# The inputs of a selective scan joined with the scan in one block, and its later step sizes made from broadcast rows

## The chip, the cores and the metric

The kernel runs on one core of one Trainium2 chip. The metric is the time of one execution on the device in microseconds; lower is better. The kernel is written engine by engine: TensorE (PE), VectorE (DVE), ScalarE (ACT), GpSimd (POOL) and SyncE (SP, which only issues transfers here) each have an instruction stream of their own and wait for each other on semaphores.

## The reference

The whole network has four layers, each a mixer and a feed-forward part, each followed by `x = layernorm(x + f(x))`, on activations of 8 sequences x 256 tokens x 128 channels. The change is in the mixer of the second layer, a selective scan:

```python
xz = x @ W_in                                   # 128 -> 2 x 256
x_inner, z = split(xz)
xc = silu(causal_depthwise_conv(x_inner, 4 taps) + conv_b)
x_ssm = xc @ W_xproj                            # 256 -> 1 + 16 + 16
delta = softplus(x_ssm[:, :1] * w_dt + b_dt)    # one raw step size a token, 256 channels
h_t = exp(delta * A) * h_{t-1} + delta * B_t * xc
y = (sum over 16 states of C_t * h_t + xc * D_param) * silu(z)
out = y @ W_out
```

## The kernel before

Each stage is one block: all engines meet at a barrier at its start and end. `stage_scan_inputs` (L1229) computes `xc` and `silu(z)` for all eight sequences, `stage_scan` (L1306) the rest. Channels lie on the 128 partitions in two halves (`c` = 0, 1), tokens along the free dimension.

Inputs, per sequence i: TensorE makes four 128x256 products in four banks (L1256; fp32, so two passes each in the trace). ScalarE copies the two x halves behind three zeros into `x_padded` (L1268), makes the first tap (L1271), the two `silu_z` (L1277) and, after VectorE's six taps (L1302, three per half, each on top of the last), the two `xc` (L1282).

Scan: one step n handles state k = n % 16 of sequence i = n // 16, 128 steps in all. ScalarE makes exp(delta * a) into a bank (`decay`, L1558, two per step), GpSimd multiplies `delta_x` with a broadcast row of B (`inject`, L1377), VectorE scans both (L1648). Even states are read out by tokens: TensorE turns them (L1434), ScalarE scales them by C (L1569), TensorE adds them up (L1463). Odd states: TensorE spreads a row of C (L1450), VectorE multiplies (L1658), TensorE adds (L1467). Rings of 4 injects, 3 decays and 4 states tie the engines together. Per sequence there are also `gate`, `step`, `stats` and `normalise` on VectorE, `project` and `turn_back` on TensorE, `rstd_of` on GpSimd.

The step sizes go by four groups of two sequences. `project_in(g)` (L1403) gives 33 rows `x_ssm`, which ScalarE (`keep`, L1526) or VectorE (group 1, L1640) copies to SBUF; `step_size(g, c)` (L1411) spreads row 0 times `w_dt` over the partitions in a bank. From that bank ScalarE takes |v + b| (`magnitude`, L1530) and VectorE max(v + b, 0) (`top`, L1613). ScalarE then takes exp(-|.|) (`below_one`, L1535) and ln(1 + .) (`log_of`, L1540), each of which needs another table, and VectorE adds both and multiplies with `xc` (`step`, L1625 and L1627). Group 0 is done before the first scan, group 1 around it, groups 2 and 3 by the dictionary `LATE` between steps 2 and 12; the logarithms of groups 1 to 3 are taken together at step 18.

SyncE stores rows 1 to 16 of a group to DRAM (`rows_out`, L1353, 32 KB) and loads them back spread over all partitions, four states of a sequence at a time (L1364, 512 KB, chunk q of 32, four buffers); chunk q waits for the injects of chunk q - 4. At its end each stage's SyncE stream runs `ready_next` (L102): it clears the semaphores of the next stage's pool and raises each by one. There are two pools used in turn, of 60 and of 36 semaphores; a stage's signals are taken from its pool in order.

Of the kernel before, what the change touches and what calls it, by code (L numbers as in the profile page):

```python
# [16 lines left out]
F32 = mybir.dt.float32  # L17
I32 = mybir.dt.int32
BF16 = mybir.dt.bfloat16
ALU = mybir.AluOpType  # L20
# [3 lines left out]
P = 128  # L24
# [1204 lines left out]
def stage_scan_inputs(nc, net, io, xc, sz):  # L1229

    with ExitStack() as ctx:
        sb = lambda name, shape: ctx.enter_context(nc.sbuf_tensor(net.name(name), shape, F32))
        PAD = NCONV - 1
        xp, acc = sb("x_padded", [P, 2, 2, PAD + L]), sb("conv", [P, 2, 2, L])
        s = open_stage(nc, net, f"clear:1 xz:{4 * B} x_padded:{2 * B} silu_z:{2 * B} first:{2 * B} taps:{2 * (NCONV - 1) * B} xc:{2 * B}")
        bank = net.bank
        seq = lambda i: slice(i * L, (i + 1) * L)
        bank_of = lambda i, m: bank[4 * (i % 2) + m]
        with nc.Block() as block:
            @block.sync  # L1240
            def _(sp):
                ready_next(sp, net)

            @block.gpsimd
            def _(pool):
                pool.memset(xp[:, :, :, :], 0.0).then_inc(s.clear.sem, 1)

            @block.tensor
            def _(pe):
                pe.wait_ge(net.ld_w, net.w_ready)  # L1250
                for i in range(B):
                    for m in range(4):
                        if i >= 2:
                            read, c = (s.x_padded, m) if m < 2 else (s.silu_z, m - 2)
                            pe.wait_ge(read.sem, read.at(0, 2 * (i - 2) + c + 1))
                        pe.matmul(bank_of(i, m)[:, 0:L], net.w_in[:, m * P:(m + 1) * P], net.xT[:, seq(i)], start=True, stop=True).then_inc(s.xz.sem, 1)  # L1256

            @block.scalar
            def _(act):
                act.wait_ge(net.ld_w, net.w_ready)  # L1260
                act.wait_ge(s.clear.sem, s.clear.at(0, 1))

                def pad(i):
                    for c in range(2):
                        act.wait_ge(s.xz.sem, s.xz.at(0, 4 * i + c + 1))
                        if i >= 2:
                            act.wait_ge(s.taps.sem, s.taps.at(0, 2 * (NCONV - 1) * (i - 1)))
                        act.activation(xp[:, i % 2, c, PAD:PAD + L], bank_of(i, c)[:, 0:L], ACT.Copy).then_inc(s.x_padded.sem, 1)  # L1268
                    for c in range(2):
                        act.wait_ge(s.x_padded.sem, s.x_padded.at(0, 2 * i + c + 1))  # L1270
                        act.activation(acc[:, i % 2, c, :], xp[:, i % 2, c, 0:L], ACT.Identity, scale=net.conv_w[:, c, 0:1], bias=net.conv_b[:, c:c + 1])\  # L1271
                            .then_inc(s.first.sem, 1)

                def gates(i):
                    for c in range(2):
                        act.wait_ge(s.xz.sem, s.xz.at(0, 4 * i + c + 3))
                        act.activation(sz[:, c, seq(i)], bank_of(i, 2 + c)[:, 0:L], ACT.Silu).then_inc(s.silu_z.sem, 1)  # L1277

                def conv(i):
                    for c in range(2):  # L1280
                        act.wait_ge(s.taps.sem, s.taps.at(0, 2 * (NCONV - 1) * i + 2 * (NCONV - 2) + c + 1))
                        act.activation(xc[:, c, seq(i)], acc[:, i % 2, c, :], ACT.Silu).then_inc(s.xc.sem, 1)  # L1282

                pad(0)
                for i in range(B):
                    gates(i)
                    if i + 1 < B:
                        pad(i + 1)
                    conv(i)

            @block.vector
            def _(dve):
                dve.wait_ge(net.ld_w, net.w_ready)
                for i in range(B):
                    at = 2 * (NCONV - 1) * i
                    for j in range(1, NCONV):
                        for c in range(2):
                            if j == 1:
                                dve.wait_ge(s.first.sem, s.first.at(0, 2 * i + c + 1))
                            else:  # L1300
                                dve.wait_ge(s.taps.sem, s.taps.at(0, at + 2 * (j - 2) + c + 1))
                            dve.scalar_tensor_tensor(acc[:, i % 2, c, :], xp[:, i % 2, c, j:j + L], net.conv_w[:, c, j:j + 1], acc[:, i % 2, c, :], ALU.mult, ALU.add)\  # L1302
                                .then_inc(s.taps.sem, 1)
# [2325 lines left out]
```

## Time and profile before

| | us |
|---|---|
| median of 3 runs | 1767.58 (1765.85 to 1769.92) |
| the profiled execution | 1780.49 |
| its span, first to last instruction | 1778.8 |
| TensorE busy in the span | 1519.8 (85%) |
| VectorE, ScalarE, GpSimd busy | 1009.0, 863.8, 632.8 |
| inputs of the scan, start to last `xc` | 538.05 to 563.62 |
| first scan instruction, last | 580.08, 810.21 |

The trace gives each instruction's start and duration, and for each idle stretch of an engine what ended it. Sums over a stage say which engine was busy, not which one decided; for that one looks at who waited for whom in that stage. "PEclk" is the granted clock of TensorE as a share of 2.4 GHz. A line such as `x4` merges neighbouring instructions of the same kind.

### The profile page before, as it was taken

The page shows a single profiled execution, that of the slowest core. Times are in us where ns is not written, and L with a number is a line of the kernel's source. Part 1 is how long each engine was busy: PE and PEld are TensorE (multiplying, and loading weights), DVE is VectorE, ACT ScalarE, POOL GpSimd, SP SyncE. Part 2 cuts the span into 40 slices and gives each one's busy share as a digit, 9 for nine tenths or more (in the row PEclk, how much of TensorE's full clock was granted, in tenths as well). Part 3 has the DMA queues.
Part 4 walks back from the last instruction along what each step waited for, and adds up shares of the span by engine and source line. Part 5 has one row for each costly group of instructions (what it writes and reads, how often), then busy time and mean ns, then how long its engine had stood idle before and what let it go on. Part 6 is the DMA issues. An engine that isn't in the chain of part 4 may idle for free. (4 is left out here: it accounts for less than half of the span.)

```text
span 1778.8 us, 31127 instructions
## 1 busy us (share of the span) xinstructions
PE 1519.8 (85%) x11198; PEld 1107.1 (62%) x11199; DVE 1009.0 (57%) x2370; ACT 863.8 (49%) x1903; POOL 632.8 (36%) x707
## 2 busy tenths in 40 slices
PE   4689978799886999996839999899996799778996
PEld 2356655466573566775837877787875476545664
DVE  6656536666375789995035554466645122535555
ACT  5455544565357677772425444544443132235552
POOL 3497603877140667772130000100013601511113
PEclk8889999899998899998959999999997899969998
DMA  7300000000000645635234000000000101300000
GB/s 219 117 10 16 13 7 2 14 13 13 13 1 14 92 65 77 78 59 121 71 89 130 1 0 1 1 1 1 1 1 6 59 26 30 37 4 2 2 2 25
DMA packets 75272, 63.65 MB, mean 36 GB/s; under 512 B 25367, under 2 KB 62790, under 8 KB 75142
## 3 DMA queue, kind: packets, MB, share of 16 engines
q1 hardware_dynamic: 65142, 53.53, 13.9%
q0 software_dynamic: 3072, 6.30, 1.8%
q10 hardware_dynamic: 6928, 2.12, 0.6%
q8 instruction: 79, 1.29, 0.3%
q14 instruction: 51, 0.42, 0.1%
HBM read 48.09 MB, written 9.57 MB: 32 GB/s over the span
## 5 line engine op out<-in xcount | busy, mean ns | idle before, releaser
L1377 POOL TENSOR_TENSOR inject<-delta_x,b_rows 128x512 f32<-128x512 f32 x128 | 159.5, 1269 | 80.2 <-DMA b_rows<-b_rows_dram 42.9
L1648 DVE TENSOR_TENSOR_SCAN state<-bank,inject 128x512 f32<-128x512 f32 x128 | 150.3, 1205 | 6.6 <-POOL inject L1377 3.3
L2085 POOL TENSOR_TENSOR ve<-mv,eps 128x1 f32<-128x1 f32 x32 | 6.1, 190 | 336.4 <-DVE mv L2233 336.4
L1558 ACT ACTIVATE bank<-delta,a_neg 128x255 f32<-128x255 f32 x256 | 109.0, 472 | 12.8 <-DVE state L1648 12.3
L3347 DVE TENSOR_REDUCE top<-bank 128x2 f32<-128x512 f32 (+1 forms) x96 | 61.8, 685 | 72.3 <-PE bank L3049 51.5
L2194 ACT ACTIVATE Z<-bank 128x512 f32<-128x512 f32 x64 | 34.7, 595 | 127.8 <-PE bank L2147 127.8
L2171 ACT ACTIVATE U<-bank 128x512 f32<-128x512 f32 x128 | 74.7, 593 | 41.8 <-PE bank L2108 40.7
L611 POOL TENSOR_TENSOR rotated<-rot_cos,rot_sin 128x512 f32<-128x512 f32 x56 | 70.8, 1269 | 52.4 <-DVE rot_sin L917 52.4
L617 POOL TENSOR_TENSOR inv_norm<-sum_sq,neghalf 128x16 f32<-128x16 f32 x28 | 82.0, 2929 | 4.2 <-POOL sum_sq L615 0.3
L1463 PEld LDWEIGHTS bank<-tabs,by_token 128*128 128x128 f32 x512 | 67.8, 196 | 24.9 <-issue 15.0
L654 PE MATMUL bank<-wqkv,hT 128*128 128x512 f32 x128 | 68.5, 665 | 14.7 <-ACT hT L815 11.3
L1569 ACT ACTIVATE by_token<-bank,c_cols 128x256 f32<-128x256 f32 x128 | 53.6, 469 | 50.8 <-PE bank L1434 50.5
L1467 PE MATMUL bank<-x_work,tabs 128*128 128x512 f32 x128 | 73.7, 658 | 0.0
L3260 ACT ACTIVATE prob<-bank 128x384 f32<-128x384 f32 x128 | 53.2, 501 | 37.0 <-PE bank L3077 37.0
L1463 PE MATMUL bank<-tabs,by_token 128*128 128x128 f32 x512 | 69.1, 279 | 0.0
L914 DVE TENSOR_TENSOR rot_cos<-bank,rope 128x512 f32<-128x512 f32 x64 | 43.8, 684 | 40.0 <-ACT squares L820 29.1
L2796 DVE TENSOR_TENSOR shared_hid<-shared_gate,bank 128x512 f32<-128x512 f32 x32 | 21.8, 686 | 65.7 <-PE bank L2648 27.4
L820 ACT ACTIVATE squares<-bank 128x512 f32<-128x512 f32 x64 | 38.0, 598 | 43.1 <-PE bank L654 23.3
L622 POOL TENSOR_TENSOR rotated<-rotated,inv_norm 128x512 f32<-128x512 f32 x56 | 57.2, 1042 | 2.2
L842 ACT ACTIVATE prob<-bank 128x512 f32<-128x512 f32 x64 | 34.7, 595 | 44.4 <-PE bank L701 44.4
L2968 POOL CAST k<-moe_w 128x512 bf16<-128x512 f32 x16 | 9.8, 610 | 116.3 <-ACT moe_w L3251 111.4
L663 PE MATMUL bank<-tabs,rotated 128*128 128x128 f32 x256 | 40.2, 292 | 12.6 <-DVE rot_sin L917 8.4
(564 smaller groups left out, 4163.2 us busy)
## 6 DMA issues: line engine op xcount, KB each, us to landing
b_rows<-b_rows_dram SPq DMA_DIRECT2D x32, 512.0 KB, 9.1
v<-v SPq DMA_DIRECT2D x32, 130.0 KB, 2.3
slots<-zero SPq DMA_DIRECT2D x10, 256.0 KB, 3.6
rows<-slots SPq DMA_DIRECT2D x10, 256.0 KB, 4.3
moe_w<-in_L_ffn_rg_dram SPq DMA_DIRECT2D x1, 2048.0 KB, 8.5
moe_w<-in_L_ffn_ru_dram SPq DMA_DIRECT2D x1, 2048.0 KB, 13.9
wqkv<-in_L_ffn_wqkv_dram SPq DMA_DIRECT2D x2, 768.0 KB
slots_out<-y SPq DMA_DIRECT2D x8, 160.0 KB, 2.1
```

Of the source, the lines that this page charges most:

```text
L611: pool.tensor_tensor(rot[:, p, m, :], rc[:, m % 2, :], rs[:, m % 2, :], ALU.add).then_inc(s.added.sem, 1)
L617: pool.tensor_tensor(flat(rn), flat(ss), net.neghalf[:, 0:2 * LH], ALU.pow).then_inc(s.inv_norm.sem, 2)
L622: pool.tensor_tensor(r, r, rn[:, m, :].unsqueeze(2).to_broadcast([P, LH, LDH]), ALU.mult).then_inc(s.roped.sem, 1)
L654: pe.matmul(to, hT[:, p, tok(t)], w[:, j * INNER:(j + 1) * INNER], start=True, stop=True).then_inc(s.qk_ps.sem, 1)
L1377: pool.tensor_tensor(dB[:, n % R, :, :], dx[:, :, seq(n)], both(b_all[:, q % 4, n % CH, :]), ALU.mult).then_inc(s.inject.sem, 1)
L1463: last = pe.matmul(sum_bank(i)[:, c * L + t * P:c * L + (t + 1) * P], hcT[:, j % RT, t, c * P:(c + 1) * P], ident, start=(k == 0 and t == ...
L1467: last = pe.matmul(sum_bank(i)[:, :], ident, flat(hc[:, j % R, :, :]), start=False, stop=(k == NS - 1))
L1558: last = act.activation(dA[n % RD][:, c, 1:L], delta[:, c, i * L + 1:(i + 1) * L], ACT.Exp, scale=a_neg[:, c, k:k + 1])
L1569: last = act.activation(hcT[:, j % RT, t, :], turn_bank[:, t * 2 * P:(t + 1) * 2 * P], ACT.Copy, scale=c_cols[:, TPB * i + t, k:k + 1])
L1648: dve.tensor_tensor_scan(flat(h[:, n % R, :, :]), flat(dA[n % RD]), flat(dB[:, n % R, :, :]), 0.0, ALU.mult, ALU.add).then_inc(s.state.sem, 1)
L2171: act.activation(U[:, m % 2, 4 * (g - 1):4 * g, :], bank[n % 2][:, :].rearrange("p (h t) -> p h t", h=4), ACT.Copy)\
L3347: dve.tensor_reduce(to, M[u % 2].rearrange("p (c k) -> p c k", c=count), AX.X, ALU.max).then_inc(s.maxed.sem, 1)
```

## The change

The two stages become one. `stage_scan_inputs` is emptied, and its work stands at the head of each engine's stream in `stage_scan`. The x products go to banks 3 to 6, each behind three columns that are zeroed once, and ScalarE and VectorE take all taps straight from the bank; `x_padded` is gone, and `conv` lies in a part of `x_tok`. The z products use the two halves of bank 7. All four `project_in` are issued among or right behind the inputs, through bank 2. Group 0's step sizes are made as before, but in the middle of the inputs. For groups 1 to 3 TensorE makes no step sizes: `rows_out` stores row 0 as well (17 rows), SyncE waits for its landing and loads row 0 spread over the partitions into `delta_x` (`step_rows`, 256 KB), ScalarE takes |row * w + b| from there at steps 5 to 10, and GpSimd makes row * w + b behind the injects 10, 12 and 14 (`top`); the max with 0 moves into `step`. `below_one` of groups 1 to 3 stands at steps 13 to 15, the logarithms at step 17. The third decay bank gets its zero column after `step(0)`. The transfers' semaphores now come from the stage's pool; as one stage fewer runs before the scan, the pools swap places, and have 44 and 60 semaphores.

```diff
-OTHER_SIGNALS = 36
+OTHER_SIGNALS = 44
-    net.pools = (net.pool, [sem(f"other_signal_{k}") for k in range(OTHER_SIGNALS)])
+    net.pools = ([sem(f"other_signal_{k}") for k in range(OTHER_SIGNALS)], net.pool)
...
 # SyncE
-                    sp.dma_start(b_dram[:, group_of(g)], ssm[1:1 + NS, group_of(g)]).then_inc(b_out[g], 16)
+                    sp.dma_start(rows_dram[:, group_of(g)], ssm[0:1 + NS, group_of(g)]).then_inc(b_out[g].sem, 16)
+                def step_rows(g):
+                    sp.wait_ge(b_out[g].sem, b_out[g].at(0, 16))
+                    sp.dma_start(dx[:, 0, group_of(g)], rows_dram[0, group_of(g)].partition_broadcast(P)).then_inc(rows_of[g].sem, 16)
...
-                    if q in (4, 6, 8):
-                        rows_out(q // 2 - 1)
+                    if q in (2, 3, 4):
+                        rows_out(q - 1)
+                        step_rows(q - 1)
...
 # GpSimd
+                def top(g):
+                    pool.wait_ge(s.abs.sem, s.abs.at(0, 2 * g + 2))
+                    for c in (1, 0):
+                        pool.tensor_scalar(dx[:, c, group_of(g)], dx[:, 0, group_of(g)], w_step[:, c:c + 1], net.b_dt[:, c:c + 1], ALU.mult, ALU.add)\
+                            .then_inc(s.top.sem, 1)
...
                 for n in range(LAST):
                     inject(n)
+                    if n in (10, 12, 14):
+                        top(n // 2 - 4)
...
 # TensorE
+                for i in range(4):
+                    inputs(i)
                 project_in(0)
+                inputs(4)
                 for c in range(2):
-                    step_size(0, c)
-                columns(early, bank[2])
+                    first_step_size(c)
+                columns(early, cc_bank)
+                inputs(5)
                 project_in(1)
-                for c in range(2):
-                    step_size(1, c)
+                inputs(6)
+                inputs(7)
+                project_in(2)
+                project_in(3)
...
 # ScalarE
+                for i in range(B):
+                    gates(i)
+                    if i + 1 < B:
+                        first_tap(i + 1)
+                    conv(i)
+                    if i == 2:
+                        keep(0)
+                    if i == 3:
+                        for c in range(2):
+                            magnitude(0, c)
+                    if i == 5:
+                        keep(1)
+                keep(2)
                 act.activation(a_exp[:, :, :], net.a_log[:, :, :], ACT.Exp).then_inc(s.a_exp.sem, 1)
...
                 below_one(0)
                 log_of(0, 1)
+                keep(3)
...
-                    if n < 2:
-                        magnitude(1, n)
-                    if n == 2:
-                        below_one(1)
...
+                    if 5 <= n < 11:
+                        magnitude(1 + (n - 5) // 2, (n - 5) % 2)
+                    if 13 <= n < 16:
                         below_one(n - 12)
-                    if n == 18:
+                    if n == 17:
                         for g in range(1, groups):
                             log_of(g, groups + g)
...
 # VectorE
-                    dve.tensor_tensor(delta[:, :, of], dx[:, :, of], delta[:, :, of], ALU.add).then_inc(s.delta.sem, 1)
+                    dve.scalar_tensor_tensor(delta[:, :, of], dx[:, :, of], 0.0, delta[:, :, of], ALU.max, ALU.add).then_inc(s.delta.sem, 1)
...
+                for i in range(B):
+                    taps(i)
+                    if i == 4:
+                        for c in range(2):
+                            first_top(c)
+                        columns(0, early, cc_bank)
...
                 step(0)
+                dve.wait_ge(s.ssm.sem, s.ssm.at(0, groups))
+                dve.memset(dA[RD - 1][:, :, 0:1], 0.0).then_inc(s.first.sem, 1)
```

## Rows read from the trace of the kernel before

**Rows 1.** Windows: us of each engine (instructions), PEclk, DMA share, GB/s.
```profile
core 0 of [0], span 1778.8 us
...
538.05:563.62 25.57, 17.68 (x64) 13.76 (x64) 20.34 (x48) 23.23 (x65) 0.95 (x1) 0.83 0.00 1
563.62:580.08 16.46, 12.06 (x24) 3.38 (x24) 4.35 (x13) 10.84 (x16) 1.30 (x2) 0.71 0.25 48
580.08:615.78 35.70, 34.34 (x146) 19.30 (x147) 29.05 (x32) 24.15 (x54) 22.86 (x19) 0.88 0.57 87
615.78:650.28 34.50, 31.75 (x149) 21.54 (x148) 26.51 (x34) 25.88 (x55) 20.41 (x18) 0.86 0.43 68
677.92:704.78 26.86, 26.86 (x151) 18.97 (x150) 26.79 (x36) 19.94 (x49) 20.77 (x18) 1.00 0.54 80
```
**Rows 2.** Timeline of the hand-over: start, us, instruction [idle before, releaser].
```profile
562.81 0.81 ACT L1282 ACTIVATE xc<-conv 128x256 f32<-128x256 f32 x2 [0.58 <-DVE conv L1302]
...
567.55 0.59 ACT L1526 ACTIVATE x_ssm<-bank 33x512 f32<-33x512 f32 x1 [2.15 <-PE bank L1403]
...
570.93 1.06 ACT L1535 ACTIVATE delta<-delta 128x1024 f32<-128x1024 f32 x1
...
572.01 1.28 ACT L1540 ACT_TABLE_LOAD   x1
...
575.33 0.67 DVE L1625 TENSOR_TENSOR delta<-delta_x,delta 128x512 f32<-128x512 f32 x1
...
577.40 2.46 ACT L1558 ACTIVATE bank<-delta,a_neg 128x255 f32<-128x255 f32 x6
578.78 4.93 POOL L1377 TENSOR_TENSOR inject<-delta_x,b_rows 128x512 f32<-128x512 f32 x4 [39.78 <-DMA b_rows<-b_rows_dram]
```
**Rows 3.** Groups by line, 580.08 to 615.78: busy, mean ns, idle before.
```profile
L1403 PE MATMUL bank<-xc,w_xproj 128*33 128x512 f32 x8 | 5.5, 829 | 0.0
...
L1411 PE MATMUL bank<-x_ssm,w_dt 1*128 1x512 f32 x8 | 4.5, 640 | 0.0
L1613 DVE TENSOR_SCALAR delta_x<-bank,b_dt 128x512 f32<-128x512 f32 x6 | 4.5, 746 | 6.2 <-ACT delta L1530 6.2
```
**Rows 4.** Timeline at the end of the first stage.
```profile
43.34 13.59 SPq L295 DMA_DIRECT2D slots<-zero  x10
...
55.61 0.60 ACT L425 ACTIVATE xT<-bank 128x512 f32<-128x512 f32 x1 [0.26 <-PE bank L344]
...
59.81 0.52 POOL L598 MEMSET hT<- 128x512 f32 x1 [19.65 <-POOLq L278]
```
**Rows 5.** Timeline: a three-operand instruction from PSUM, and the taps.
```profile
532.26 0.48 DVE L1205 SCALAR_TENSOR_TENSOR z<-bank,b,both 128x256 f32<-128x256 f32 x1 [0.52 <-PE bank L1139]
...
544.55 17.82 DVE L1302 SCALAR_TENSOR_TENSOR conv<-x_padded,conv_w,conv 128x256 f32<-128x256 f32 x40 [0.93 <-ACT conv L1271]
```
**Rows 6.** Timeline: TensorE's inputs, C columns, and a projection, at full clock.
```profile
551.29 1.99 PE L1256 MATMUL bank<-xT,w_in 128*128 128x256 f32 x8 [0.66 <-ACT silu_z L1277]
...
570.11 1.06 PE L1415 MATMUL bank<-tabs,x_ssm 33*128 33x16 f32 x8
...
599.21 1.91 PE L1403 MATMUL bank<-xc,w_xproj 128*33 128x512 f32 x4
```
**Rows 7.** Groups of GpSimd by line and shape, whole span.
```profile
L1377 POOL TENSOR_TENSOR inject<-delta_x,b_rows 128x512 f32<-128x512 f32 x128 | 159.5, 1269 | 80.2 <-DMA b_rows<-b_rows_dram 42.9 <-DVE state L1648 37.3
...
L622 POOL TENSOR_TENSOR rotated<-rotated,inv_norm 128x512 f32<-128x512 f32 x56 | 57.2, 1042 | 2.2
...
L1056 POOL TENSOR_TENSOR both<-x_work,xT 128x256 f32<-128x256 f32 x8 | 5.9, 732 | 0.1
...
L2992 POOL TENSOR_SCALAR x_tok<-x_tok,t_mv,t_rstd 128x128 f32<-128x128 f32 x6 | 5.0, 833 | 0.0
```
**Rows 8.** L1364 (b_rows) issued 570.1 to 571: issues ns, and landing.
```profile
L1364 SPq DMA_DIRECT2D b_rows<-b_rows_dram x3: 388/502/670, 569.8 to 570.7; - x3
...
DMA to landing us min/median/max: 8.9/14.8/21.0
```
**Rows 9.** L1353 (`rows_out`), all four: landing after issue.
```profile
DMA to landing us min/median/max: 1.6/16.5/22.1
```

More of the change, by code:

```diff
@@ L1229, in stage_scan_inputs @@
 def stage_scan_inputs(nc, net, io, xc, sz):
[L1231 to L1263, printed above, removed]
-                    for c in range(2):
[L1265 to L1303, printed above, removed]
@@ L1306, in stage_scan @@
+    pass
 def stage_scan(nc, net, io, xc, sz):
@@ L1313, in stage_scan @@
         R, RD, RT, LAG = 4, 3, 3, 4
-        CH = 4
+        CH, PAD = 4, NCONV - 1
         CHUNKS = LAST // CH
@@ L1322, in stage_scan @@
         st, mv, ve, rstd = sb("n_st", [P, NT, 6]), sb("n_mv", [P, NT, 2]), sb("n_ve", [P, NT]), sb("n_rstd", [P, NT])
-        b_dram = nc.dram_tensor(net.name("b_rows_dram"), [NS, T], F32, kind="Internal").ap()
-        sem = lambda name: ctx.enter_context(nc.semaphore(net.name(name)))
-        b_out, b_in = [sem(f"b_out{g}") for g in range(groups)], [sem(f"b_in{q}") for q in range(4)]
-        s = open_stage(nc, net, f"first:1 a_exp:1 a_ready:1 skip_w:1 ssm_ps:{groups} ssm:{groups} dt_ps:{2 * groups} abs:{2 * groups} tail:{2 * groups} top:{2 * groups} "
+        acc = net.x_tok[:, T // 2:T].rearrange("p (r c t) -> p r c t", r=2, c=2)
+        w_step = sb("w_step", [P, 2])
+        rows_dram = nc.dram_tensor(net.name("rows_dram"), [1 + NS, T], F32, kind="Internal").ap()
+        s = open_stage(nc, net, f"clear:1 xz:{4 * B} silu_z:{2 * B} tap0:{2 * B} taps:{2 * (NCONV - 1) * B} xc:{2 * B} w_step:16 b_out0:16 b_out1:16 b_out2:16 b_out3:16 b_in0:16 b_in1:16 b_in2:16 b_in3:16 step_rows1:16 step_rows2:16 step_rows3:16 "
+                       f"first:1 a_exp:1 a_ready:1 skip_w:1 ssm_ps:{groups} ssm:{groups} dt_ps:2 abs:{2 * groups} tail:{2 * groups} top:{2 * groups} "
                        f"delta:{B} dx:{B} cc_ps:2 c_cols:2 inject:{LAST} decay:{LAST} state:{LAST} "
@@ L1498, in _ @@
                         add(n - LAG)
-                    if n in LATE:
-                        what, g, c = LATE[n]
-                        if what == "in":
-                            project_in(g)
-                        else:
-                            step_size(g, c)
                     if n == 14:
-                        pe.wait_ge(s.top.sem, s.top.at(0, 2 * groups))
-                        pe.wait_ge(s.abs.sem, s.abs.at(0, 2 * groups))
+                        pe.wait_ge(s.ssm.sem, s.ssm.at(0, groups))
                         columns(late, y_bank)
@@ L1605, in _, with taps, first_top @@
                 dve.wait_ge(net.ld_w, net.w_ready)
[L1606 to L1613 removed]
+                def taps(i):
+                    at = 2 * (NCONV - 1) * i
+                    for j in range(1, NCONV):
+                        for c in range(2):
+                            if j == 1:
+                                dve.wait_ge(s.tap0.sem, s.tap0.at(0, 2 * i + c + 1))
+                            else:
+                                dve.wait_ge(s.taps.sem, s.taps.at(0, at + 2 * (j - 2) + c + 1))
+                            dve.scalar_tensor_tensor(acc[:, i % 2, c, :], x_bank(i, c)[:, j:j + L], net.conv_w[:, c, j:j + 1], acc[:, i % 2, c, :], ALU.mult, ALU.add)\
+                                .then_inc(s.taps.sem, 1)
+                def first_top(c):
+                    dve.wait_ge(s.dt_ps.sem, s.dt_ps.at(0, c + 1))
+                    dve.wait_ge(s.abs.sem, s.abs.at(0, c + 1))
+                    dve.tensor_scalar(dx[:, c, group_of(0)], dt_bank[c][:, :], net.b_dt[:, c:c + 1], None, ALU.add).then_inc(s.top.sem, 1)
                 def columns(k, of, bank_of):
@@ L1689, in _ @@
                         read(n - 1)
-                    if n < 2:
-                        top(1, n)
-                    if n - 1 in LATE and LATE[n - 1][0] == "step":
-                        top(*LATE[n - 1][1:])
                     if n == 15:
```

110 lines of the change are left out of this document (60 added, 50 removed).

## The prediction

> **What bounds the kernel now.** The windows by stage come first [rows 1]. The change touches the scan's inputs and the scan, which start at 538 us of a span of 1778.8 us. In the fifth window, one sequence of 16 steps in the steady state takes 26.86 us with TensorE busy for all of it and VectorE for 26.8; the diff edits nothing there. What differs from the steady state is the head: 16.5 us from the end of the inputs to the first scan, then 35.7 us for the first sequence and 34.5 for the second. The timeline of the hand-over [rows 2] shows why: behind the last convolution stands a chain of table loads and long activations on ScalarE, and even then the first scan waits for GpSimd, whose first `inject` waits for broadcast rows. The groups by line inside the first sequence [rows 3] show TensorE with 5.5 us of projections (L1403) and 4.5 us of step sizes (L1411) among the scan's own matmuls, in a window where it is busy 34.3 of 35.7 us. The execution took 1780.5 us, the median of the three timed runs is 1767.6; all differences below are made against this one execution and then put on the median.
>
> **Stage signals.** The two pools change places and sizes. Behind the first stage SyncE raises 60 signals one by one, not 36. There SyncE is last: its transfers are issued until 56.93 us, ScalarE ends at 56.21, and the next stage starts at 59.81 [rows 4]. So 36 increments and the barrier fit in 2.88 us, at most 0.08 each; 24 more cost 0 to 1.9 us, and I take **+1.7**. In the other stages SyncE has few transfers or none behind which the signals stand, and the other engines' work covers them; without that cover a stage would pay the same 1.7.
>
> **The inputs.** Per sequence VectorE has six tap instructions, started 17.82/40 = 0.445 us apart, 2.67 us in all; this already sets the pace. With their source in PSUM they should cost the same: the three-operand instruction of this width that reads PSUM takes 0.48 us [rows 5]. ScalarE loses the 16 copies to `x_padded`; only the first was on the path, so the first tap starts some 0.5 us earlier. What is new is TensorE's order: `project_in(0)` stands before `inputs(4)`, the two first step sizes and eight `columns` passes before `inputs(5)`, `project_in(1)` before `inputs(6)`. At full clock these are 1.91 us, 2 x 1.12 + 1.06 = 3.3 us, and 1.91 us [rows 3, 6]. The x banks are free one sequence ahead, a pair of x matmuls takes about 1.0 us (1.99 for four [rows 6]) and its first tap some 0.6; laid out sequence by sequence, VectorE then waits 0.7, 1.7 and 0.6 us. It fills most of the 1.7 with `first_top` and `columns(0)`, work it formerly did later. The last convolution ends at 563.62 - 0.5 + 3.0 + 0.5 (silu queued behind `keep`) = 566.6: **+3.0**. Bounds: 0 if nothing waits; and +14 if TensorE is at 1.2 GHz throughout, since its work in the last four sequences, 4 x 2.0 + 4 x 1.91 + 3.3 = 18.9 us, would double, with some 5 us of slack.
>
> **The hand-over.** After the last silu: `keep(2)` 0.6, exp table 1.28, exp 1.06, ln table 1.28, ln 1.06, the sum on VectorE 0.7 (0.67 now, three-operand in future), the product 0.7, exp table again 1.28, first decay 0.8, together 8.8, with 0.5 for `a_exp` and hops 9.3 us against 16.5 [rows 1, 2]. Gone are the waits for the projection and the step sizes, VectorE's copy of the second group's rows, and GpSimd's wait for rows: these are now sent at about 552, and a broadcast of 512 KB lands 8.9 us after its issue [rows 8]. The first `inject` (1.27) lies beside the table load and the decays. First scan at 566.6 + 9.3 = 575.9 against 580.1: **-4.2** for the two parts together.
>
> **The first sequence.** TensorE loses 5.5 + 4.5 us and VectorE six `top` of 0.75, 4.5 us [rows 3]: they would be busy for 24.3 and 24.6 us. ScalarE is busy for 24.2 us now and takes on one more exp of 1.06. GpSimd becomes the longest: 16 times 1.27 is 20.3 us, and six new instructions, a multiply and an add with two pointers on 128x512. No row has that shape. Nearest in kind is L2992, the two-pointer form on 128x128, mean 0.83 us. Nearest in width are L1377 (1.27) and L1056, half as wide (0.73), so 2.1 ns a column; 384 more columns add 0.8 to 0.83. I take 1.6 each, 9.6 together; bounds are 1.04 (L622, the cheapest 128x512) and 4 x 0.83 = 3.3 [rows 7]. `top(1)` needs both magnitudes of group 1, which ScalarE gives at its steps 5 and 6, so GpSimd idles some 1.5 us. From the product at 573.6: 17 injects 21.6 + 9.6 + 1.5 = 32.7, so the seventeenth scan can start at 606.3. Behind each `top` stand the next injects, and VectorE waits for them.
> The Trainium skill (GPSIMD Engine Reference, Engine selection) would leave such arithmetic to VectorE, and its section on performance versus the Vector engine gives 769 ns for 512 elements in the best case. The 0.83 us of a quarter of that width in this trace [rows 7] speaks against so low a price; by it the six would cost 4.6 us and VectorE, not GpSimd, would pace the sequence.
>
> **The transfers.** SyncE's queue gets longer: behind each `rows_out(g)` stand a wait for its landing and `step_rows(g)` of 256 KB, ahead of the next b_rows. Three b_rows issued within 1 us landed after 8.9, 14.8 and 21.0 us, 6.1 us apart [rows 8], and a `rows_out` took 1.6 us alone and up to 22.1 behind them [rows 9]. `rows_out(1)`, at 562.4, stands behind q1 and lands near 570; each round then takes 3.1 + 6.1 us and a landing, 11 to 12 us: the step rows of group 2 near 585, q3 near 592, the step rows of group 3 near 598, q4 near 605. They are wanted at 589, 593, 594 and 606. The third makes ScalarE wait 3 to 5 us, with two decays in hand. I charge **+2** for this and for TensorE's low clock in the first pairs: seventeenth scan at 608.2 against 615.8, **-7.6** in all for both stages. Behind it only the ln step moves, one iteration earlier: 0.
> The Trainium skill (DMA: Bandwidth & Descriptors, Why a DMA increments its semaphore by 16 and not by 1) says that a transfer is spread over the largest number of engines up to 16 that divides its slowest dimension. By it the 17 rows of the new `rows_out`, where there were 16, go through a single engine; no row here shows such a transfer, and rival (c) bounds it from rows.
>
> **Sum.** +1.7 - 7.6 = **-5.9 us**: 1774.6 for the profiled execution, 1761.7 on the median. Its own range, with the signals at 0 to 1.9 and a `top` at 1.04 to 2.2, is 1758 to 1765.
>
> **Rivals.** (a) The six instructions are cheap, 1.04 us, and the rows are in time: GpSimd saves 3.4 and the +2 mostly goes: -10, 1757.5. For it: L622. Against it: L2992. (b) They cost 2.5 to 3.3 us: 5.4 to 10 us more on GpSimd, which eats the first sequence's gain; 1767 to 1770. For it: nothing shows that the price of the two-pointer form is not by width. (c) The transfers decide, slower. Place: `magnitude(3)` on ScalarE behind `step_rows(3)`, and q4. Each engine's share of 512 KB is 32 KB in 6.1 us [rows 8]; if the 34 KB of `rows_out` took that on one engine, a round would be 17 to 18 us, the step rows of group 3 would land near 614 and q4 near 620, ScalarE would stand from 594 on and the seventeenth scan would start near 622: +6 + 1.7 = +8, 1775.5. It decides once a `rows_out` takes over 4 us. Against it: 1.6 us for 32 KB alone [rows 9]. (d) TensorE at 1.2 GHz through the inputs: +14 in place of +3, 1773. Against it: a mean clock of 0.83 in that window now, and more matmuls in it later [rows 1]. (e) The move does not do what it says: the first sequence stays at 35.7 because its loop of turns and scalings paces it, then -4.2 + 1.7 = -2.5, 1765. For it: TensorE was 96% busy. Against it: 10 us of that leave.
>
> **Chances.** Forecast 0.40, (a) 0.15, (b) 0.17, (c) 0.12, (d) 0.06, (e) 0.10. About 0.2% (3.5 us) is what a measurement of this kernel can tell. Faster: 0.85 of the forecast's cases, (a), and a quarter of (b) and (e), 0.34 + 0.15 + 0.07 = 0.56. Slower: (c) and (d), 0.18. Same: 0.26. The range, 1755 to 1772, leaves out (c), most of (d) and a little of (a).
>
> **What would show it.** A gap 1.7 us wider before L598; the first scan near 577.6 with that shift, and some 32 us of 16 steps behind it; six new GpSimd instructions of about 1.6 us; taps at 0.48 us; the sequences from the third on at 26.9 us as before. It is wrong if an `inject` or a `magnitude` waits on a DMA for over 5 us, if a tap from PSUM takes over 0.6 us, or if the steady sequences change.

## The result, and the profile after

The changed kernel takes 1756.33 us (median of 5 runs, 1755.63 to 1757.85), beside 1767.58 us (5 runs, 1765.85 to 1771.36) of the kernel before on the same chip: a ratio of 0.9932, interval 0.9919 to 0.9945 (about 9.7 to 14.3 us). The medians are 11.25 us apart. The forecast was 5.9 us less, 1761.7, with a range of 1755 to 1772. Here and below, executions far above the rest of their kernel are in no ratio: there were two, one of e6 (1781.8 us) and one of e9 (2509.5).

The windows by stage of the changed kernel, cut at the same events as [rows 1] (us of each engine, PEclk, DMA share, GB/s; the first is the inputs up to the last `xc`):

```profile
538.74:566.81 28.07, 26.78 (x88) 15.93 (x88) 21.75 (x55) 21.32 (x54) 0.00 (x0) 0.91 0.16 35
566.81:576.07 9.26, 1.88 (x4) 0.36 (x4) 1.63 (x4) 8.01 (x11) 2.26 (x2) 0.74 0.51 89
576.07:604.33 28.26, 26.25 (x132) 18.75 (x132) 25.19 (x27) 24.86 (x56) 26.65 (x25) 0.84 0.51 88
604.33:640.51 36.18, 33.33 (x148) 22.49 (x147) 26.67 (x35) 25.90 (x55) 20.73 (x18) 0.81 0.57 77
668.25:695.12 26.87, 26.87 (x151) 18.97 (x150) 26.80 (x36) 19.95 (x49) 20.77 (x18) 1.00 0.53 80
```

The first scan starts 4.0 us earlier (576.07 against 580.08), the first sequence is 7.4 us shorter (28.26 against 35.70), the second 1.7 us longer (36.18 against 34.50), and the steady sequence is the same. The last scan starts at 800.53 against 810.21, 9.7 us earlier, although the block began 0.3 us later. From the start of the last instruction of the stage before (537.71, and 537.40 in the kernel before) to the last scan it takes 262.8 us against 272.8. That is 10.0 us less, at the low side of the interval above.

The two profiled spans differ by 24.3 us, though (1778.8 and 1754.5), so some of that has another source. The stage with the largest difference behind the scan, in the windows of the kernel before (first line) and of the changed one (second):

```profile
1363.30:1558.90 195.60, 161.22 (x778) 109.51 (x778) 64.38 (x182) 49.45 (x111) 64.08 (x65) 0.93 0.16 36
```
```profile
1350.00:1535.20 185.20, 158.75 (x778) 109.43 (x778) 64.42 (x182) 49.92 (x111) 64.03 (x65) 0.93 0.17 38
```

The numbers of instructions are the same (778 on TensorE, 182 on VectorE) and nothing of the diff is there. 10.4 us of the 24.3 lie in this stage; that they are no effect of the change is tested by running both kernels again, below.

**The hand-over**, timeline of ScalarE, VectorE, GpSimd and SyncE's queue, to be laid beside [rows 2]:

```profile
566.00 0.81 ACT L1489 ACTIVATE xc<-x_tok 128x256 f32<-128x256 f32 x2 [0.58 <-DVE x_tok L1592]
...
566.71 0.57 ACT L1493 ACTIVATE x_ssm<-bank 33x512 f32<-33x512 f32 x1
567.30 1.28 ACT L1530 ACT_TABLE_LOAD   x1
...
568.73 1.04 ACT L1508 ACTIVATE delta<-delta 128x1024 f32<-128x1024 f32 x1
...
569.79 1.28 ACT L1513 ACT_TABLE_LOAD   x1
571.09 1.06 ACT L1513 ACTIVATE delta<-delta 128x1024 f32<-128x1024 f32 x1
...
572.25 0.69 DVE L1610 SCALAR_TENSOR_TENSOR delta<-delta_x,delta 128x512 f32<-128x512 f32 x1 [3.21 <-ACT delta L1513]
572.98 0.69 DVE L1612 TENSOR_TENSOR delta_x<-delta,xc 128x512 f32<-128x512 f32 x1
573.68 0.06 DVE L1632 MEMSET bank<- 128x2 f32 x1
573.80 1.28 ACT L1544 ACT_TABLE_LOAD   x1 [1.18 <-DVE bank L1632]
573.81 7.39 POOL L1315 TENSOR_TENSOR inject<-delta_x,b_rows 128x512 f32<-128x512 f32 x6 [37.58 <-DVE delta_x L1612]
```

The 2.15 us for the projection is gone, and GpSimd's first `inject` is released by VectorE's product, no longer by a transfer. What is left is a chain on ScalarE with one hole: it waits 1.18 us for a zero column (L1632) that VectorE writes only after the product.

**The first sequence**, groups by line from 576.07 to 604.33 (busy us, mean ns, then idle before):

```profile
L1315 POOL TENSOR_TENSOR inject<-delta_x,b_rows 128x512 f32<-128x512 f32 x19 | 24.4, 1313 | 0.0
L1639 DVE TENSOR_TENSOR_SCAN state<-bank,inject 128x512 f32<-128x512 f32 x17 | 19.8, 1205 | 2.3 <-ACT bank L1544 2.3
L1503 ACT ACTIVATE delta<-delta_x,b_dt,w_step 128x512 f32<-128x512 f32 x6 | 4.9, 813 | 0.0
L1327 POOL TENSOR_SCALAR delta_x<-delta_x,w_step,b_dt 128x512 f32<-128x512 f32 x6 | 4.6, 770 | 1.6 <-ACT delta L1503 1.6
```

The six new GpSimd instructions (L1327) took 0.77 us each. GpSimd never waited for a transfer here, nor did ScalarE; SyncE's queue did all the waiting for transfers (its waits by line from 550 to 606, total us, times, longest):

```profile
SPq L1288 <- DMA rows_dram<-x_ssm: 22.2, 3, 8.9
SPq L1284 <- ACT x_ssm L1493: 20.3, 2, 12.9
...
SPq L1302 <- DMA rows_dram<-x_ssm: 2.6, 1, 2.6
```

### The profile page after: what moved, and what is told of

Read it like the earlier page. It is cut to its first block and busy times, and to the rows that moved or that the text cites. A ratio compares the mean times of both kernels' runs of the same rounds, so it can differ in the third digit from the quotient of the medians.

```text
span 1754.5 us, 31069 instructions
## 1 busy us (share of the span) xinstructions
PE 1509.9 (86%) x11186; PEld 1104.7 (63%) x11187; DVE 1004.8 (57%) x2367; ACT 860.9 (49%) x1888; POOL 636.9 (36%) x712
## 5 line engine op out<-in xcount | busy, mean ns | idle before, releaser
L1419 PEld LDWEIGHTS bank<-tabs,by_token 128*128 128x128 f32 x512 | 68.7, 198 | 25.2 <-issue 15.1
L914 DVE TENSOR_TENSOR rot_cos<-bank,rope 128x512 f32<-128x512 f32 x64 | 43.8, 685 | 40.3 <-ACT squares L820 29.1
L622 POOL TENSOR_TENSOR rotated<-rotated,inv_norm 128x512 f32<-128x512 f32 x56 | 57.2, 1042 | 2.2
```

The source lines that it names most:

```text
L622: pool.tensor_tensor(r, r, rn[:, m, :].unsqueeze(2).to_broadcast([P, LH, LDH]), ALU.mult).then_inc(s.roped.sem, 1)
L1419: last = pe.matmul(sum_bank(i)[:, c * L + t * P:c * L + (t + 1) * P], hcT[:, j % RT, t, c * P:(c + 1) * P], ident, start=(k == 0 and t == ...
```

## The experiments

Each was timed beside the kernel before on its chip; ratios are to that kernel. Three chips were used: one for e1 to e4, one for e5 to e8, one for e9 to e12. They differ by some 10 us (medians of the kernel before: 1775.1, 1767.9 and 1776.6), and intervals are about 0.2% wide on either side, so most verdicts rest on the trace: inputs (from the start of the last instruction of the stage before, 537.4 in before and 537.7 in after, to the last `xc`; 26.2 us in before), hand-over (to the first scan; 16.5 in before), and the sequences.

| | ratio [interval] | inputs | hand-over | sequence 1, 2 |
|---|---|---|---|---|
| after | 0.9932 [0.9919, 0.9945] | 29.1 | 9.26 | 28.26, 36.18 |
| e5, the same again | 0.9951 [0.9928, 0.9973] | 29.1 | 9.26 | 28.32, 36.21 |
| e1 `top` on VectorE | 0.9983 [0.9964, 1.0002] | 32.3 | 9.26 | 33.02, 34.87 |
| e10 the same, wait moved | 0.9954 [0.9936, 0.9971] | 29.1 | 9.26 | 33.00, 34.92 |
| e2 TensorE's load put back | 1.0000 [0.9990, 1.0011] | 30.5 | 9.26 | 35.68, 35.72 |
| e3 rows sent late | 1.0023 [1.0002, 1.0045] | 29.1 | 13.04 | 39.35, 34.96 |
| e6 x products first | 0.9966 [0.9944, 0.9987] | 32.9 | 9.26 | 28.11, 34.65 |
| e7 signals by GpSimd | 0.9939 [0.9920, 0.9958] | 30.5 | 9.26 | 28.92, 32.96 |
| e8 earlier zero column | 0.9926 [0.9905, 0.9947] | 29.2 | 8.53 | 28.69, 33.54 |
| e9 first taps before group 0 | 0.9952 [0.9932, 0.9973] | 30.2 | 10.33 | 28.93, 32.91 |
| e11 e7 + e9 + e8's column | 0.9945 [0.9926, 0.9964] | 30.2 | 9.60 | 30.17, 36.21 |
| e12 logarithms at step 18 | 0.9940 [0.9919, 0.9961] | 29.1 | 9.26 | 28.25, 36.15 |

**e2: TensorE's load put back.** All else as after; the results are thrown away.

```diff
+                    if n in (2, 8):
+                        for c in range(2):
+                            pe.matmul(y_bank[0:XP, :], net.w_xproj[:, c, :], xc[:, c, group_of(1)], start=(c == 0), stop=(c == 1))
+                    if n in (4, 6, 10, 12):
+                        pe.matmul(y_bank[:, :], net.w_dt[:, 0:P], ssm[0:1, group_of(1)], start=True, stop=True)
```

> The kernel after, with the matmuls that it took out of the first sequence put back on TensorE as dead work: two projections at steps 2 and 8 and four step-size products at steps 4, 6, 10, 12, all into an unused bank; nobody waits for them. Theory A (TensorE's queue paced the first sequence before): 10 us of matmuls come back and the first sequence grows from 28.3 by 6 to 9 us, to 34 to 37. Theory B (the waits between engines for step sizes and the late rows paced it, TensorE's busy time was cover): under +3 us, first sequence at most 31.

The first sequence took 35.68 us, to 0.02 the 35.70 of before, and on the clock the whole gain was gone. Its window, beside the third line of [rows 1]:

```profile
576.29:611.97 35.68, 34.31 (x146) 19.45 (x147) 25.56 (x26) 25.14 (x56) 27.82 (x25) 0.88 0.61 85
```

TensorE is busy for 34.3 us in both. GpSimd does 27.8 us of work here against 22.9 before and it makes no difference. So the 10 us of projections and step sizes (L1403 and L1411 of [rows 3]) in TensorE's in-order queue, between the turns and rows of C that VectorE and ScalarE wait for, are enough to bring the old length back. The low clock does not explain it: TensorE was at 1.2 GHz for 8.4 us of this sequence in e2 and in before, 8.9 in after. Early rows and `top` off VectorE, which e2 still has, gain nothing in this sequence while TensorE is that full.

**e1 and e10: the six instructions on VectorE.** In `top` the engine changes, with its place in the order of steps (10, 12, 14).

```diff
-                    if n in (10, 12, 14):        # GpSimd, behind inject(n)
-                        top(n // 2 - 4)
+                    if n in (10, 12, 14):        # VectorE, before scan(n)
+                        top(n // 2 - 4)
...
+                dve.wait_ge(s.w_step.sem, s.w_step.at(0, 16))   # e1: ahead of the first tap; e10: behind taps(5)
```

> The kernel after, with the six `top` instructions of groups 1 to 3 on VectorE, behind the same steps, not on GpSimd. In the kernel after they took 0.76 us each on GpSimd (forecast: 1.6) and the first sequence took 28.3 us. Theory A (TensorE's removed matmuls are what shortened the first sequence, and VectorE has room in it): the six cost VectorE some 0.4 to 0.75 us each, the first sequence stays within 28 to 30 us, total 0 to +2 us against the kernel after. Theory B (taking `top` off VectorE is the gain, since VectorE paces): +3 to +4.5 us, first sequence 31.5 to 33.

> As e1_top_vector (the six operations that form x W + b of the later groups, on VectorE instead of GpSimd), but VectorE's wait for the loaded weights stands behind the taps of sequence 5 instead of ahead of the first. Theory A (what made e1's inputs block 32.3 us instead of 29.1 was that wait alone): the block is back at 29.0 to 29.4 us, the first sequence stays at 32.5 to 33.5 us against 28.3, so the last scan comes some 4 to 5 us later than in the kernel after, ratio to the kernel before 0.996 to 0.997. Theory B (VectorE has something else in that block): the block stays above 31 us and the ratio at 0.998 or above.

e1's inputs took 3.2 us longer, which muddied it: VectorE waited there for the loaded weights. With the wait moved (e10) they are back at 29.1, and the first sequence stays at 33.0, 4.7 us longer than on GpSimd. VectorE is the engine with the most work then, 30.3 us against 25.2 in after (the window of the sequence, groups of VectorE by shape in it, and L1676 alone):

```profile
578.37:611.37 33.00, 28.16 (x131) 19.81 (x132) 30.27 (x32) 25.27 (x56) 23.30 (x19) 0.81 0.65 86
...
L1639 DVE TENSOR_TENSOR_SCAN state<-bank,inject 128x512 f32<-128x512 f32 x16 | 18.9, 1208 | 2.3 <-ACT bank L1542 2.3
L1676 DVE TENSOR_SCALAR delta_x<-delta_x,w_step,b_dt 128x512 f32<-128x512 f32 x6 | 5.8, 1006 | 0.0
...
L1676 DVE TENSOR_SCALAR delta_x<-delta_x,w_step,b_dt x6: 515/1006/1500, 595.6 to 605.4; 128x512 f32<-128x512 f32 x6
```

Each of the six took from 0.515 to 1.5 us (minimum, median, maximum in the last line), on GpSimd in after 0.763 to 0.774. TensorE was at 1.2 GHz for 3.6 us more of this sequence than in after, but VectorE did not wait for it any longer (2.6 us in all, against 2.9). Taking the load off TensorE alone thus gains 2.7 us of the 7.4 (35.7 to 33.0), and taking `top` off VectorE alone gains nothing (e2); it takes both. e10's gain on the clock is 0.46%; on the same chip e12, which is after with its logarithms one step later, has 0.60%.

**e3: rows sent late.** SyncE waits for all convolutions before the first `rows_out`, as it did when the scan was a block of its own.

```diff
+                sp.wait_ge(s.xc.sem, s.xc.at(0, 2 * B))
                 rows_out(0)
```

> The kernel after, but SyncE stores and loads no row of B before the last convolution of the inputs is done, as the kernel before did. Theory A (the early rows are worth only what GpSimd waited at its first inject): first scan 1 to 3 us later, and another 0 to 2 us in the first sequence. Theory C (the rate of the b_rows transfers, 6.1 us each, was the second thing that paced the first sequence before): the injects wait for q1, q2 and q3 again and `magnitude` for its step rows; first scan +2 to +3, first sequence +5 to +10 us, total +7 to +13 us.

The hand-over took 3.8 us more, and the first sequence 39.35 us, 11.1 more: both above what theory C expected. GpSimd's timeline there shows who was late:

```profile
578.98 4.94 POOL L1316 TENSOR_TENSOR inject<-delta_x,b_rows 128x512 f32<-128x512 f32 x4 [42.34 <-DMA b_rows<-rows_dram]
584.23 4.96 POOL L1316 TENSOR_TENSOR inject<-delta_x,b_rows 128x512 f32<-128x512 f32 x4 [0.32 <-DMA b_rows<-rows_dram]
594.41 3.72 POOL L1316 TENSOR_TENSOR inject<-delta_x,b_rows 128x512 f32<-128x512 f32 x3 [5.21 <-DMA b_rows<-rows_dram]
```

In the sequence GpSimd waited 6.5 us for transfers of B, and ScalarE 6.0 for step rows; TensorE, idle meanwhile, was at 1.2 GHz for 22.3 us of it, against 8.9 in after. How the 11.1 us divide between waits and clock stays open. But without two chunks on their way before the hand-over the change gains nothing: the head start of the rows, which the one block allows, is needed. What the missing barrier is worth by itself was not measured.

**e4 and e5: both kernels again, unchanged.**

> The kernel before once more, for a second profile. In the first profile its execution took 1780.5 us where its timed runs took 1767.6, and the stage of the second set of experts took 195.6 us from its start to its end, against 185.2 in the kernel after. Theory: that stage's 10 us belong to that one execution; here it takes 185 to 187 us, the scan's stages take the same as in the first profile within 2 us, and the profiled execution is near 1768. Rival: the 10 us are a property of the kernel before, and show again.

> The kernel after once more, beside the kernel before on the same chip. The first pair of profiles came from executions that differ by 10 us in the stage of the second experts, which the change does not touch; a second profile of the kernel before showed the same 196 us there. Theory: the gain lies between 537 us and the last scan instruction, 10 us in total (first scan at 576, first sequence 28.3, second 36.2), and the stage of the second experts takes what it takes in the kernel before on this chip (195 to 196 us); ratio 0.993 to 0.995. Rival: that stage is faster in the kernel after, 185 us again, and the total gain on this chip is above 15 us.

In the stage shown above e4 took 196.2 us and e5 188.0, on two chips. Both expectations named another time for it (185 to 187, and 195 to 196), and both missed. e12, whose code there is that of after, took 194.8 on the chip where the kernel before has a median of 1776.6:

```profile
1349.60:1544.40 194.80, 160.35 (x778) 109.28 (x778) 64.47 (x182) 49.53 (x111) 64.18 (x65) 0.93 0.16 36
```

The other traces, cut at the same events, settle it. On the chip of e1 to e4 the kernel before (e4) takes 196.2 us, and three kernels that have the change's code there 194.1 to 196.1; the chip of e5 to e8 gives 185 to 188, that of e9 to e12 192 to 195. So the stage goes by the chip, and the difference of the spans there is not the change's. The block of the scan, in contrast, repeats: 272.8 and 272.9 us in before and e4, 262.8, 263.0 and 262.8 in after, e5 and e12, on at least three chips.

**e6 and e9: other orders of the inputs.** VectorE waits before its taps at 552.6, 557.6 and 561.3 (1.10, 0.60 and 1.25 us). e6 sends TensorE's x products of a sequence ahead of group 0's projection, the z products behind; e9 moves group 0's work behind later sequences on all three engines.

```diff
 # e6
-                project_in(0)
-                inputs(4)
+                inputs(4, x_of)
+                project_in(0)
+                inputs(4, z_of)
+                inputs(5, x_of)
                 for c in range(2):
                     first_step_size(c)
...
 # e9, TensorE
-                project_in(0)
                 inputs(4)
+                project_in(0)
+                inputs(5)
                 for c in range(2):
                     first_step_size(c)
                 columns(early, cc_bank)
-                inputs(5)
-                project_in(1)
                 inputs(6)
                 inputs(7)
+                project_in(1)
```

> The kernel after with TensorE's inputs split: the two x products of sequences 4, 5 and 6 are issued ahead of the projection (or step sizes) that stands before them, the z products behind it. Theory (VectorE's waits of 1.1, 0.6 and 1.25 us before the taps of sequences 4 to 6 come from x products queued behind a projection): the last convolution ends 1.5 to 3 us earlier (at 564 to 565.5 instead of 566.8), the first scan moves by as much, total -1.5 to -3 us. Rival (ScalarE's queue, with its waits for the projections, holds the first taps up anyway): under 0.7 us.

> Only the order in the inputs block is changed: on TensorE the projection of group 0 comes behind inputs of sequence 4, the first step sizes and early columns behind those of sequence 5, the projection of group 1 behind those of 7; on ScalarE keep(0) and the two magnitudes come one sequence later and keep(1) behind the loop; on VectorE the first tops and the columns come behind the taps of sequences 6 and 5. In the kernel after, VectorE stands idle before the taps at 552.64, 557.57 and 561.33 (1.10, 0.60 and 1.25 us). Theory A (those waits come from work of group 0 that stands ahead of a first tap in an in-order queue): the block from its first matmul to the last xc falls from 29.1 us to 26.5 to 27.8 us and the first scan comes 1 to 2.5 us earlier, if the hand-over stays at 9.3 (it may give 0.5 back, since keep(1) now stands ahead of the exponential); the ratio to the kernel before is about 0.992. Theory B (ScalarE has no room there: its own work sets the block, and the waits only move): the block stays at 28.8 to 29.3 us and the ratio at 0.993 to 0.995.

Both failed: 32.9 and 30.2 us against 29.1. In e6 the projection comes 1.1 us later (550.21 against 549.09), and so does `keep(0)`, which stands ahead of the next first tap in ScalarE's queue and waits 2.61 us for it; the idle time only moved and grew (timelines of ScalarE and of VectorE in e6):

```profile
552.15 0.59 ACT L1497 ACTIVATE x_ssm<-bank 33x512 f32<-33x512 f32 x1 [2.61 <-PE bank L1358]
...
553.76 2.50 DVE L1596 SCALAR_TENSOR_TENSOR x_tok<-bank,conv_w,x_tok 128x256 f32<-128x256 f32 x6 [2.32 <-ACT x_tok L1482]
```

In e9 the waits moved as well, to VectorE's columns (1.68) and the taps behind them (timeline of VectorE in e9), and a second `keep` ahead of the exponential, with its wait for the projection, lengthened the hand-over by 1.07:

```profile
556.30 2.50 DVE L1591 SCALAR_TENSOR_TENSOR x_tok<-bank,conv_w,x_tok 128x256 f32<-128x256 f32 x6 [0.97 <-ACT x_tok L1478]
560.49 0.23 DVE L1602 COPY c_cols<-bank 128x64 f32<-128x64 f32 x1 [1.68 <-PE bank L1367]
562.30 0.48 DVE L1591 SCALAR_TENSOR_TENSOR x_tok<-bank,conv_w,x_tok 128x256 f32<-128x256 f32 x1 [1.58 <-ACT x_tok L1478]
```

In both, and in e11 with e9's order (30.2), TensorE's granted clock fell to 1.2 GHz for 6.8 us of the second half of the inputs, as it did in no run with 29.1 or 29.2 us. Of the other kernels, e2 and e7 had 3.4 us of it there, and 30.5 us of inputs (e1 too, beside its wait). What share of e6's and e9's loss is the clock and what the order stays open.

**e7, e8, e11: what the trace of after points to.** e7 lets GpSimd raise the first stage's 60 signals in place of SyncE; e8 writes the zero column between the two halves of the first `step` and moves `keep(2)` behind the exponential; e11 has e7, e9 and e8's column.

```diff
 # e7
-                ready_next(sp, net)
+                ready_next(pool, net)        # at the end of GpSimd's stream
 # e8
+                    if i == 0:               # in step, between the sum and the product
+                        dve.wait_ge(s.ssm.sem, s.ssm.at(0, groups))
+                        dve.memset(dA[RD - 1][:, :, 0:1], 0.0).then_inc(s.first.sem, 1)
```

> The kernel after with the 60 signals of the next stage raised by GpSimd, which is idle at the end of the first stage, and no longer by SyncE behind its transfers. Theory (that step of the forecast: SyncE is last there, and the 24 more signals cost 1.4 us): the second stage starts at 56.5 to 57.5 us, not 59.4, and all behind it moves by 2 to 3 us. Rival (the stage's end waits for something else that ends then): no change.

> The kernel after with two moves in the hand-over: `keep(2)` behind the exp of group 0, off the head of ScalarE's chain (0.57 us), and the zero column of the third decay bank between the two halves of `step(0)`, so that the last table load can start when the step sizes are there and not 0.8 us later. Theory (the chain of ScalarE sets the first scan): first scan 0.6 to 1.3 us earlier relative to the last convolution (9.26 us before it now). Rival (the first `inject`, which follows the product on VectorE by 1.3 us, takes over): 0.5 to 0.7 us at most.

> The order of e9_order, with SyncE's 60 signals of the first stage raised by GpSimd (as e7_pool_raises) and VectorE's wait for the last kept projection put between the two halves of its first step (as e8_handover, without that one's move of keep(2)). If the three add: 2.1 us from the stage's start, 0.4 to 0.7 from the hand-over and 1 to 2.5 from the block, so 3.5 to 5 us below the kernel after, about 1752 us, ratio to the kernel before 0.990 to 0.991. If they cover each other (something else that ends at the same time, such as the transfers at the stage's start): 1 to 2 us below it, ratio 0.992 to 0.993.

Each did its step: e7's second stage started at 57.28 instead of 59.40, e8's hand-over took 8.53 instead of 9.26 us. By their ratios (0.9939 and 0.9926) neither can be told from the change. On their chip the change itself is e5, median 1760.27: e7's is 2.2 us lower (1758.12), within the noise, and e8's 5.9 lower (1754.35), with means 4.6 apart, interval 0.8 to 8.5. In the traces e8's block is 3.8 us shorter than e5's, 0.7 of it in the hand-over and 2.7 in the second sequence, where TensorE's clock was low for 6.8 us less. e11, which has e7, e9's order and the zero column, is no better at 0.9945. Its trace says where the earlier start went: the block began 1.9 us sooner than in after, and 1.1 us in the inputs, 0.3 in the hand-over and 1.9 in the first sequence were given back. So e8 is a candidate for a faster kernel, by one pair out of several and mostly through the clock; no other version came out faster.

**e12: the logarithms at step 18.**

```diff
-                    if n == 17:
+                    if n == 18:
```

> The three logarithms of the later groups at scan 18 instead of 17, all else as after. In the kernel after, the second sequence took 36.2 us against 34.5 before; in it ScalarE loads a function table at 610.2, computes the three logarithms, loads the other table back, and VectorE stands idle 5.15 us before the scan at 616.97. Theory A (ScalarE's place in the order costs it: the logarithms run into the low clock of TensorE and the scans behind them find no decay ready): one scan later the idle moves by one scan but stays 5 us, and the second sequence is 35.5 to 36.5 us; time within 1 us of the kernel after, ratio 0.993 to 0.995. Theory B (the logarithms are too early by one scan, before ScalarE's two decays ahead are spare): the idle falls by 1 us or more and so does the time, ratio 0.992.

The second sequence took 36.15 us against 36.18: one step later costs the same; other places were not tried. In e12 the wait of 5.15 us before the scan of after at 616.97 becomes 3.05 (timelines of VectorE, after and e12), and the rest turns up between the steps around it:

```profile
616.97 1.22 DVE L1639 TENSOR_TENSOR_SCAN state<-bank,inject 128x512 f32<-128x512 f32 x1 [5.15 <-issue]
```
```profile
617.46 1.22 DVE L1639 TENSOR_TENSOR_SCAN state<-bank,inject 128x512 f32<-128x512 f32 x1 [3.05 <-ACT bank L1544]
```

What the second sequence does go with is TensorE's clock. Between the seventeenth and the thirty-third scan the records show 1.2 GHz for 13.7 us in after, e5, e11 and e12 (36.15 to 36.21 us), 12.3 in e2 (35.72), 9.8 to 10.2 in before, e4, e1, e3, e6 and e10 (34.50 to 34.96), and 6.8 in e7, e8 and e9 (32.91 to 33.54). Windows of e7 and e12 over that sequence; the granted clock is the third number from the end:

```profile
603.94:636.90 32.96, 29.86 (x148) 20.41 (x147) 26.10 (x34) 25.92 (x55) 20.73 (x18) 0.90 0.57 80
```
```profile
604.04:640.19 36.15, 33.32 (x148) 22.46 (x147) 27.01 (x35) 25.79 (x55) 20.80 (x18) 0.81 0.66 76
```

The same 148 matmuls take 3.5 us more of TensorE's time, and the sequence 3.2 us more. This is a comparison of kernels whose code there is nearly the same, not an experiment on the clock itself; what makes it fall was not found.

## Why the prediction came out as it did

The time is inside the range and the sign is right, but the mechanism of the sum was half right, and what happened is nearer to rival (a) (1757.5, cheap instructions and rows in time, given 0.15) than to the forecast (1761.7, given 0.40). The sum's own range, 1758 to 1765, missed; only the wider one holds the result. Two misses partly cancel, which is luck: up to the last scan the first sequence came out 4.0 us better than forecast and the later ones 1.8 worse. Another 1.5 are the signals, which did not show in this trace.

- **Stage signals, +1.7.** Right in size: the interval from SyncE's last issue (55.11) to the next stage (59.40) is 4.3 us against 2.9 of [rows 4], so the 24 extra signals cost 1.4 us. In this execution the transfers ahead of them were issued 1.8 us earlier, and the stage even began 0.4 sooner. The mechanism holds: e7, without SyncE's signals, starts 2.1 us sooner. That gain can't be told from noise on the clock.
- **The inputs, +3.0.** Right: the last `xc` at 566.81, forecast 566.6. VectorE's waits were 1.10, 0.60 and 1.25 us against 1.7, 0.6 and 0.7 by the layout; the taps from PSUM took 0.48 us each.
- **The hand-over, 9.3.** Right: 9.26; the first scan at 576.07, forecast 575.9. e3 confirms the part that hung on the rows' head start: without it 13.0 us.
- **The first sequence.** Here the prediction failed in size: about 32 us forecast, 28.3 measured. The step "I take 1.6 each, 9.6 together" was wrong: 0.77 us each, 4.6 together, below the lower bound of 1.04. The bound came from instructions that read two tensors (L622, L1377, L1056 of [rows 7]); this one reads one tensor and two pointers a partition. The argument from L2992 (0.83 for a quarter of the width) took the price of a narrow instruction as a floor for its width. The Trainium skill (GPSIMD Engine Reference, Performance versus the Vector engine) gave 769 ns for 512 elements in the best case. The six measure 763 to 774, so its figure was right here and the objection to it was not. The preference of the Trainium skill (GPSIMD Engine Reference, Engine selection) for VectorE in elementwise work did not hold in this kernel, where e10 is 4.7 us longer in this sequence; its remark there that one-input work is roughly at line rate on GpSimd fits the 0.77 us.
- **The transfers and the clock, +2.** No engine but SyncE waited for a DMA in the first sequence. The order of arrival was misread: [rows 8] is a queue of three 512 KB chunks issued at once, while in the new order each `step_rows` is issued behind a wait and landed in 3.1 to 3.2 us, for group 2 near 582 and for group 3 near 591, where 585 and 598 were forecast. Rival (c) "decides once a `rows_out` takes over 4 us"; SyncE waited up to 8.9 us for one and it decided nothing, because the rows were wanted later still. Alone, the first 17-row transfer kept SyncE waiting 2.6 us, where the first one of 16 rows kept it waiting 1.2 in before. That goes in the direction of the Trainium skill's rule on the spread over engines (DMA: Bandwidth & Descriptors), but one such case doesn't prove it.
- **The second sequence, 0.** Wrong by +1.7. Its code is nearly as before, but TensorE's clock was low for 13.7 us of it against 9.9. That the clock is the cause was not tested.
- **Rivals.** (b) and (e) fell with the trace: 0.77 us, and 28.3 us of first sequence. By its own prices (b) would reach 1772, not 1770, and the low end of the sum's range would be 1756.6, not 1758; both slips are small. (e)'s remark that TensorE was 96% busy was the right reading: e2 shows that its queue is enough for the old length, e10 that relieving it is not enough for the new one. (d) did not occur in after; 3.4 us of low clock in the inputs of e2 and e7 went with 1.4 us more there.

The signs named in advance: taps at 0.48 us, no `inject` or `magnitude` waiting for a DMA, and steady sequences at 26.87 us (26.86 before) came as forecast. The six new instructions of 1.6 us and 32 us for 16 steps did not.

In sum to the last scan: +3.2 (end of the inputs) -7.2 (hand-over) -7.4 (first sequence) +1.7 (second) +0.1 (third) = -9.7, where -5.9 was forecast. The clock's 11.25 has an interval of about 2.3 us either way.

## What to carry to other kernels

When an in-order engine is nearly full in a warm-up stretch, take out of its queue whatever another resource can supply: here 10 us of matmuls in it became three broadcast loads that no computing engine waited for and 4.6 us on an engine that had room. Look at the next fullest engine at the same time: with the new work on VectorE the sequence gained 2.7 us, on GpSimd 7.4. Price a new instruction by rows that read as many tensors as it does, and do not let a narrow instruction's price scale up. And before a second rearrangement is worked out to the microsecond, find out what each idle stretch waits for: e6, e9 and e12 moved idle time instead of removing it.

## What was not expected of the hardware

VectorE and GpSimd slow each other down in some pairings. In the changed kernel, while GpSimd ran two `inject`, VectorE ran the two halves of `step` (timelines of VectorE and of GpSimd):

```profile
590.12 0.91 DVE L1610 SCALAR_TENSOR_TENSOR delta<-delta_x,delta 128x512 f32<-128x512 f32 x1
591.05 1.64 DVE L1612 TENSOR_TENSOR delta_x<-delta,xc 128x512 f32<-128x512 f32 x1
```
```profile
590.45 3.38 POOL L1315 TENSOR_TENSOR inject<-delta_x,b_rows 128x512 f32<-128x512 f32 x2
```

The same two take 0.69 each in the hand-over with GpSimd idle, and an `inject` 1.26 elsewhere; here 0.91, 1.64 and 1.69. The scans (1.19 to 1.23 us) and `x_work` (0.65 to 0.69, L1649) kept their times beside `inject` in every trace. Those two read one operand from a bank; the VectorE instructions that were slowed read none from a bank. That this is what decides was not tested. e10's instruction on VectorE, from 0.515 to 1.5 us, shows the same effect. GpSimd's stayed within 11 ns in after, but not everywhere: in e2, e3 and e11 four of eighteen took 1.18 to 1.21 us, each while VectorE ran one half of `step`. The slowing is not new with the change: the first half of `step` takes some 1.46 us in the steady sequences, before and after.

A small two-input GpSimd instruction costs almost what a wide one-input one does: 0.73 us at 128x256 [rows 7] against 0.77 at 128x512.
